# Audio tower on one core: small and large weight loads of the opening on two queues, and the first batch ahead of the weight preparation

## The reference

```
h = tokenizer(x)                        # frames * window -> DFT -> power -> mel
                                        #   -> log(mel + 1e-6) @ dct.T @ w_proj + b_proj
n = layernorm(h)
h = h + attention_block(n)              # rmsnorm * norm1_w; q, k, v = n @ wq, wk, wv (8 heads)
                                        # scores = q.k + (q.w_pos).basis + u.k + (v.w_pos).basis
                                        # softmax, @ v, @ wo + bo; rmsnorm; gelu(@ w1 + b1) @ w2 + b2
h = h + moe(layernorm(h))               # 16 experts, capacity 1000, plus a shared expert
```

## Time and profile before

| | us |
|---|---|
| median of 3 runs | 2097.63 |
| lowest and highest of the 3 | 2095.09, 2100.26 |
| the profiled execution | 2095.16 |
| its span, first to last instruction | 2093.5 |
| PE busy | 1937.0 (93% of the span) |
| DVE, ACT, POOL busy | 1351.9, 1070.5, 702.5 |

### The profile page before, as it was taken

One profiled execution on the slowest core, in us unless ns is written; L12 is line 12 of the kernel. 1 busy time (PEld: TensorE's weight loads), 2 busy tenths in 40 slices (PEclk: granted clock), 3 DMA queues, 4 the chain that ended last, 5 costly groups with the idle time before them and its releaser, 6 DMA issues. The chain is left out here.

```text
span 2093.5 us, 46401 instructions
## 1 busy us (share of the span) xinstructions
PE 1937.0 (93%) x13428; PEld 1660.4 (79%) x13428; DVE 1351.9 (65%) x3700; ACT 1070.5 (51%) x2588; POOL 702.5 (34%) x587
## 2 busy tenths in 40 slices
PE   2899999999999999999958899899999999999997
PEld 2788888888888788888747777788888888888886
DVE  2578878878878877877847777454555555555531
ACT  2687887887887887787732221222222222222221
POOL 0022222222222222222210002366566655566653
PEclk9899999999999999999979999999999999999999
DMA  5556656666666666666726333244445444444452
GB/s 153 161 160 173 192 168 172 191 169 173 189 170 173 187 172 173 186 174 173 194 74 162 98 102 97 56 82 88 85 88 98 90 84 78 78 78 81 81 94 20
DMA packets 318048, 272.95 MB, mean 130 GB/s; under 512 B 80732, under 2 KB 305326, under 8 KB 317998
## 3 DMA queue, kind: packets, MB, share of 16 engines
q1 hardware_dynamic: 238878, 235.53, 41.4%
q0 software_dynamic: 70656, 30.65, 9.9%
q10 hardware_dynamic: 8464, 6.15, 0.9%
HBM read 151.25 MB, written 120.54 MB: 130 GB/s over the span
## 5 line engine op out<-in xcount | busy, mean ns | idle before, releaser
L1208 POOL DMA_INDIRECT out<-ff_y,ff_idxs x128 | 261.8, 2045 | 244.7 <-DVE ff_y L1481 187.6
L1263 ACT ACTIVATE ff_sg<-ffp_g 128x500 f32<-128x500 f32 x192 | 112.9, 588 | 397.2 <-PE ffp_g L1593 397.2
L1195 POOL DMA_INDIRECT ff_xg<-xs_d,ff_idxg x128 | 204.3, 1596 | 284.5 <-issue 271.2
L524 ACT ACTIVATE sb_prob<-sb_ssb,sb_mx 125x250 f32<-125x250 f32 x512 | 253.1, 498 | 61.0 <-DVE sb_rinv L614 33.1
L1605 PE MATMUL ffp_d<-ff_wd,ff_wide 128*125 128x192 f32 x1536 | 261.2, 327 | 16.2 <-DVE ff_wide L1468 15.4
L1468 DVE TENSOR_TENSOR ff_wide<-ff_sg,ffp_u 128x500 f32<-128x500 f32 x192 | 129.4, 674 | 222.1 <-PE ffp_u L1593 222.1
L1605 PEld LDWEIGHTS ffp_d<-ff_wd,ff_wide 128*125 128x125 f32 x1536 | 247.8, 188 | 20.0 <-issue 18.4
L1593 PE MATMUL ffp_g<-ff_xsp,ff_wsp 128*128 128x500 f32 x960 | 251.2, 392 | 1.9 <-DVE ff_xsp L1345 1.6
L1593 PE MATMUL ffp_u<-ff_xsp,ff_wsp 128*128 128x500 f32 x960 | 248.9, 389 | 0.0
L822 PE MATMUL ps_qps<-sb_hsp,sb_wsp 128*128 128x250 f32 x1280 | 186.8, 293 | 31.5 <-DVE sb_hsp L728 22.8
L1593 PEld LDWEIGHTS ffp_g<-ff_xsp,ff_wsp 128*128 128x128 f32 x960 | 179.8, 189 | 39.8 <-issue 2.4
(11 more groups left out here) (189 smaller groups left out, 3562.6 us busy)
## 6 DMA issues: line engine op xcount, KB each, us to landing
bias_d<-sb_rsb SPq DMA_DIRECT2D x256, 219.6 KB
sb_bsk<-bias_d SPq DMA_DIRECT2D x256, 218.8 KB
hx_d<-sb_hx SPq DMA_DIRECT2D x32, 336.0 KB
sb_hxl<-hx_d SPq DMA_DIRECT2D x32, 336.0 KB
ff_wd<-WdT SPq DMA_DIRECT2D x16, 576.0 KB, 4.9
xs_d<-sb_xs SPq DMA_DIRECT2D x32, 238.0 KB
bias_d<-sb_rsb SPq DMA_DIRECT2D x256, 25.5 KB
sb_bsk<-bias_d SPq DMA_DIRECT2D x256, 25.4 KB
```

The lines of the kernel that those rows point to most:

```text
L524: a.activation(prob[:, s % 2, t], ssb[:, s % 2, t], ACT.Exp, bias=mx[:, s % 2, t:t + 1], scale=-1.0, accum_out=rs[:, t, s:s + 1]).then_inc ...
L1195: g.indirect_dma_start(xg[:, t], None, xs_d[:, :], bass.IndirectOffsetOnAxis(idxg[:, t:t + 1], 0), bounds_check=last).then_inc(gat, 16)
L1208: g.indirect_dma_start(out_d[:, :], bass.IndirectOffsetOnAxis(idxs[:, t:t + 1], 0), y[:, t], None, bounds_check=last, compute_op=ALU.add). ...
```

## The change

ACT issues 14 loads at its very start: eight small ones of the first stage (`dft`, `dct`, `w_proj`, `b_proj`, `melT` twice, `ident`, `n1w`) on a new semaphore `t_ld`, then `wqT`, `v` and the four of `w_pos`, still on `w_ld`. SP keeps the other 26, now with the large weights first and the biases `b2`, `bo` last; it waits for two memsets in place of three. POOL clears the tiles in another order, and waits for `w_ld` only after its first power. PE makes `wmel` first (`mel_mm`, `mel_in`), runs the first batch's DFT, mel and `wmel` products on `t_ld` alone, and then folds. ACT and DVE do their parts of the weight preparation inside the first batch, behind `hx` and behind the statistics. The folded products move from `tps` and `cps` to `cps` and `otps`, since `tps` now holds the first batch. The wait for `ini` (8 now) stands ahead of the first `qk`. In the other rounds nothing moves.

```
 def opening(bt):
     return isinstance(bt, int) and bt == 0
@@ sync: the order of SP's loads
-loads = [ident, dft, mel, mel, dct, wproj, b_proj, wqT, wo, w2, gate, n1w, n2w, b1, u, v]
...
+loads = []
+for name, (first, end) in COLS.items():
+    loads += [(wraw[:, 0, cols], w[name][0:128])]
+    loads += [(wraw[64 * i:64 * i + 64, 1, cols], w[name][128:D]) for i in range(2)]
...
-            sp.wait_ge(z_set, 3)
+            sp.wait_ge(z_set, 2)
             for dst, src in loads:
                 sp.dma_start(dst, src).then_inc(w_ld, 16)
+            sp.wait_ge(z_set, 7)
@@ scalar
+            for dst, src in ((dft[:], w["dft"]), (dct[:], w["dct"]), (wproj[:], w["w_proj"]), (wmel[MELS:MELS + 1], w["b_proj"]),
+                             (mel[0:BINS], w["melT"]), (mel[BINS:2 * BINS], w["melT"]), (ident[:], w["ident"]), (n1w[:], w["n1w"])):
+                act.dma_start(dst, src).then_inc(t_ld, 16)
+            act.wait_ge(z_set, 1)
+            act.dma_start(wqT[:], w["wqT"].rearrange("(p r) n -> r p n", r=128)).then_inc(w_ld, 16)
...
             a.preload_act_table_set(EXP_SET)
-            act.wait_ge(w_ld, W_LOADS)
+            act.wait_ge(t_ld, T_LOADS)
...
                         a.activation(hx[:, :, 0:D], bank2(tps, D, TP), ACT.Copy).then_inc(t_ev, 1)
+                        if opening(bt):
+                            weights_high()
@@ vector
                         v.tensor_scalar(t_v[:, NT:2 * NT], t_inv[:], EPS, None, ALU.add).then_inc(t_ch, 1)
+                        if opening(bt):
+                            weights_low()
@@ tensor
-            pe.wait_ge(w_ld, W_LOADS)
+            pe.wait_ge(t_ld, T_LOADS)
+            pe.wait_ge(z_set, 7)
+            m(qps[1][0:MELS, 0:D], dct[:], wproj[:], start=True, stop=True).then_inc(mel_mm, 1)
...
-            pe.wait_ge(ini, 9)
...
                 if p == 0:
+                    if opening(b):
+                        pe.wait_ge(ini, 8)
                     pe.wait_ge(t_ev, T_USES * (b + 1))
...
                         ins.then_inc(t_mm, 1)
+                        if opening(bt):
+                            fold()
```

More of the change, by code:

```diff
@@ L205, in tower @@
         zero_st = sem("zero_st")
+        t_ld = sem("t_ld")
+        mel_mm = sem("mel_mm")
+        mel_in = sem("mel_in")
         fold_mm = sem("fold_mm")
@@ L319, in load_shared @@
                     sp.dma_start(sh.xraw[half * 64:half * 64 + 64, 0, 1], xnT_d[128:D, 0:CHUNK]).then_inc(sh.x_ld[0], 16)
[L321 to L324, removed]
+            loads = []
+            for name, (first, end) in COLS.items():
+                cols = slice(first, end)
+                loads += [(wraw[:, 0, cols], w[name][0:128])]
+                loads += [(wraw[64 * i:64 * i + 64, 1, cols], w[name][128:D]) for i in range(2)]
+            for i in range(2):
+                for r in range(2):
+                    loads += [(braw[64 * r + 32 * i:64 * r + 32 * i + 32, i, 0:ND], w["basis"])]
+            loads += [
+                (ucol[:], w["u"]),
                 (wo[:], w["wo"].rearrange("(k p) n -> p k n", p=128)),
@@ L333, in _ @@
                           (bb[:, t, D:2 * D], w["bo"].partition_broadcast(TP))]
[L334 to L341, removed]
             def load_frames(b):
@@ L412, in _ @@
             g.memset(logmel[:], 1.0).then_inc(z_set, 1)
-            g.memset(vz[:], 0.0).then_inc(z_set, 1)
             g.memset(tiny[:], 1e-6).then_inc(z_set, 1)
             g.memset(power[:], -0.5).then_inc(z_set, 1)
-            pool.wait_ge(w_ld, W_LOADS)
+            g.memset(zeros[:], 0.0).then_inc(z_set, 1)
+            g.memset(vz[:], 0.0).then_inc(z_set, 1)
             pool.wait_ge(z_set, 7)
@@ L464, in _, with weights_high @@
             a = nc.scalar
+            for dst, src in ((dft[:], w["dft"]), (dct[:], w["dct"]), (wproj[:], w["w_proj"]), (wmel[MELS:MELS + 1], w["b_proj"]),
[3 more added lines that the diff above has]
+            act.dma_start(wqT[:], w["wqT"].rearrange("(p r) n -> r p n", r=128)).then_inc(w_ld, 16)
+            act.dma_start(vcol[:], w["v"]).then_inc(w_ld, 16)
+            for i in range(2):
+                for r in range(2):
+                    act.dma_start(wpz[64 * i:64 * i + 64, :, r, i], w["w_pos"].rearrange("(p i d) n -> i d p n", i=2, d=DK)[i]).then_inc(w_ld, 16)
             a.preload_act_table_set(EXP_SET)
-            act.wait_ge(w_ld, W_LOADS)
+            act.wait_ge(t_ld, T_LOADS)
             act.wait_ge(z_set, 7)
[L469 to L474, removed]
+            def weights_high():
+                act.wait_ge(w_ld, W_LOADS)
+                for k in range(2):
+                    a.activation(wsp[:, 2 * k, 0:ALL_COLS], wraw[:, k], ACT.Copy).then_inc(w_hi, 1)
+                act.wait_ge(fold_mm, 1)
+                for k in range(2):
+                    for i in range(2):
+                        a.activation(pos_cols(slice(0, 128), 2 * k, i), folded(i, k), ACT.Copy).then_inc(w_hi, 1)
             def shared_high():
@@ L566, in _, with weights_low @@
             v = nc.vector
-            dve.wait_ge(w_ld, W_LOADS)
+            dve.wait_ge(t_ld, T_LOADS)
             dve.wait_ge(z_set, 7)
[L569 to L579, removed]
+            dve.wait_ge(mel_mm, 1)
+            v.tensor_copy(wmel[0:MELS], qps[1][0:MELS, 0:D]).then_inc(mel_in, 1)
+            def weights_low():
+                dve.wait_ge(w_ld, W_LOADS)
+                v.tensor_copy(bz[:], braw[:]).then_inc(ini, 1)
+                for k, half in ((0, slice(0, 128)), (1, slice(64, 128))):
+                    dve.wait_ge(w_hi, k + 1)
+                    v.tensor_tensor(wsp[half, 1 + k, 0:ALL_COLS], wraw[half, k], wsp[half, 2 * k, 0:ALL_COLS].bitcast(F32), ALU.subtract).then_inc(ini, 1)
+                dve.wait_ge(fold_mm, 1)
+                v.tensor_copy(cq[:], qps[0][:, 0:PAIRS]).then_inc(ini, 1)
+                dve.wait_ge(w_hi, 6)
+                for k, half in ((0, slice(0, 128)), (1, slice(64, 128))):
+                    for i in range(2):
+                        v.tensor_tensor(pos_cols(half, 1 + k, i), folded(i, k)[half], pos_cols(half, 2 * k, i).bitcast(F32), ALU.subtract).then_inc(ini, 1)
             def pt_copy(b, h):
@@ L699, in body @@
                             v.bn_stats(t_stats[:, t], hx[:, t, 0:D]).then_inc(t_ch, 1)
-                        apart(dve, READY, (t_ch, b0 + 2))
+                        apart(dve, (t_ld, T_LOADS), (t_ch, b0 + 2))
                         for t in range(NT):
@@ L736, in _, with fold @@
             m = nc.tensor.matmul
-            pe.wait_ge(w_ld, W_LOADS)
[L738 to L746, removed]
-            pe.wait_ge(ini, 9)
-            pe.wait_ge(z_set, 7)
+            pe.wait_ge(t_ld, T_LOADS)
+            pe.wait_ge(z_set, 7)
+            m(qps[1][0:MELS, 0:D], dct[:], wproj[:], start=True, stop=True).then_inc(mel_mm, 1)
+            def fold():
+                pe.wait_ge(w_ld, W_LOADS)
+                for p in range(PAIRS):
+                    for k in range(2):
+                        for i in range(2):
+                            rows = slice(64 * i, 64 * i + 64)
+                            m(folded(i, k)[:, p], wqT[rows, p, k * 128:(k + 1) * 128], wpz[rows, p, 0, i], start=True, stop=True)
+                for p in range(PAIRS):
+                    ins = m(qps[0][:, p:p + 1], wpz[:, p].rearrange("d r i n -> d (r i n)"), vcol[:, p:p + 1], start=True, stop=True)
+                ins.then_inc(fold_mm, 1)
             def transposes(ps, src, s):
@@ L894, in body @@
                         pe.wait_ge(t_ev, T_USES * bt + 2)
+                        if opening(bt):
+                            pe.wait_ge(mel_in, 1)
                         ps = bank2(tps, D, TP)
```

12 lines of the change are left out of this document (7 added, 5 removed).

## The result

| | before | after |
|---|---|---|
| median, us | 2098.95 (4 runs, 2095.09 to 2100.44) | 2083.36 (4 runs, 2079.59 to 2088.32) |
| the profiled execution | 2095.16 | 2088.32 |
| its span | 2093.5 | 2086.7 |

The ratio is 0.9939, 95% interval 0.9922 to 0.9955: 12.8 us faster, with 9.4 to 16.4 as its interval. The two medians of the table lie 15.6 apart, which is inside it. The median of 2083.36 stands at the forecast of 2083. The profiled execution is the slowest of the four and shows only 6.8 us of gain in its span, so its opening is read first and its far end apart.

The account below looks back on a forecast made before the run. PE is busy 93% of the span; the opening's loads were taken as bound by issue on one queue. First `qk` 14.4 us earlier, less 0.7 for late frames, gives 13.7: from the median 2083.9, set at 2083, range 2076 to 2091.

Parts of the forecast that it names:

- The issue on SP: Opening, SP's queue: its 26 loads cost 14.2 us, the last issued at 16.0 in place of 23.08.
- `w_ld` full: Opening: all weight loads landed at 20.1, range 18.0 to 22.5, with `bb` last on few engines; chance 0.60 for 19 to 21.5.
- its two rows of 58 and 101: Profiled GB/s while `bb` loads were under way; four `bb` loads would take 6.5 us at 58 or 3.7 at 101.
- The small loads: Opening, ACT's queue: eight small loads, issued by 3.9, have landed at 6 to 8.
- the rival: Small loads queue beside large ones, `t_ld` fills at 16 or later, first stage sticks out: gain 5 to 9; chance 0.06.
- The preparation: Weight preparation after the loads: 8.16 us less 0.8 for the `wmel` product, so 7.4; `ini` full at 27.5.
- The end of the first stage: From weight preparation to the first `qk`: 4.42 us as before, so `qk` starts at 31.9, 14.4 earlier.
- The frames behind the zeros: Second batch's frames, queued behind 3.9 MB of zeros, land at 36 to 38.5 for use at 35.3: 0.7 lost.
- The sum: Whole kernel: 14.4 gained at the first `qk` less 0.7 for late frames, 13.7 us.
- shared issue: Rival: both queues share descriptor generation, `w_ld` full at about 24.6, gain 9.9, 2087.7 us; chance 0.11.
- Loads hidden at 18.0: Rival: loads land right behind their issue, `w_ld` full at 18.0 with `bb` hidden, gain 15.5, 2082 us; chance 0.13.
- The clock: Rival: PE's clock stays lower for longer from `qk` on, work takes 1.75 times as long, kernel slower; chance 0.04.

Follow-up runs that it names:

- Experiment 6: Changed kernel with nine loads used only by later stages (`wo`, `w2`, `gate`, `n2w`, `b1`, four `bb`) on their own semaphore, same order: 2082.69 us, 0.9948 of before.
- experiment 8: Changed kernel with late loads on their own semaphore and second frames ahead of the zeros: 2078.40 us (0.9924 of before); again 2077.92 beside the changed kernel's 2078.94.
- experiment 3: Changed kernel with all 40 loads on SP in the old order, so only the first batch moves ahead of weight preparation: 2087.65 us, 0.9959 of before.
- experiment 4: Changed kernel with the four 125-row loads of `b2` and `bo` first in SP's order instead of last: 2085.04 us, 0.9939 of before.
- Experiment 7: Changed kernel with only the second batch's frames loaded ahead of the zeros: 2082.79 us, 0.9953 of before.
- experiment 2: Changed kernel with weight preparation again ahead of the first batch, so only the loads are split over two queues: 2092.45 us, 0.9977 of before.

## Why the prediction was right, point by point

**The issue on SP**: right, 16.53 for 16.0. ACT's issues ended at 8.5 for 7.5: the eight small ones took until 4.4 for 3.9, and the four `w_pos` 3.0 for 2.6. Its table load hid under the wait for the small loads.

**`w_ld` full**: forecast 20.1, range 18.0 to 22.5; six profiles with this order of loads show 20.50 to 22.07. The mechanism was the one priced, `bb` last on few engines, and 20.1 was its mis-sized term, by 1.0. From the first `bb` issue at 14.42 it took 6.66; less the 1.5 that the prediction counts until the first bytes move, 375 KB in 5.16 us are 73 GB/s. That lies between its two rows of 58 and 101, nearer the slower. The faster row may hold other bytes, too: SP began to issue the first `w_pos` load at 10.82, so it isn't sure that at 11.5 `bb` was alone under way. Experiment 6 shows what the tail costs: loads needed early are in at 16.95 (15.18 and 17.30 in experiment 8), so 3 to 6 us of waiting are for biases that nobody reads yet. The share of 0.35 from 16 to 17 agrees with 5 of 16 engines, as the Trainium skill, "DMA: Bandwidth & Descriptors", § "Why a DMA increments its semaphore by 16 and not by 1", gives for 125 rows; the 18.6 that its figure for an engine led to is earlier than all six profiles, and the measurement decides. Whether the zeros, which are issued from 16.53 on, slowed its end was not separated.

**The small loads**: forecast 6 to 8, measured 9.12 to 9.67. The last was issued at 3.94, so it took over 5 us to land while the engines were filling up with the large weights. This looks like the mechanism of the rival, in small, but it isn't shown: in experiment 3 the same load, issued by SP at 6.69 with fewer large ones about, took 4.1 too. It cost nothing: the power was ready at 19.1, 2.0 before the weights. Even in experiment 4, where they came in at 14.41, the first stage did not stick out: `qk` is 2.65 later there, and `w_ld` 2.66.

**The preparation**: 7.35 for 7.4 (21.08 to 28.43). **The end of the first stage**: 4.52 for 4.42. `qk` at 32.95 for 31.9, and the difference of 1.0 is that of `w_ld`.

**The frames behind the zeros**: right in its mechanism. The prediction let the frames land at 36 to 38.5 for a use at 35.3, a wait of 0.7 to 3.2, and took 1.76 of idle time off it; that left a loss of 0 to 1.5, of which it took 0.7. The frames came at 36.7 to 38.1, as forecast, though their issue alone took 2.83 where it took 0.56 before. But `qk`, and with it their use, was 1.0 later. So the waits were 0.29, 0.86 and 1.69, each below 1.76, and the loss is 0: the second `qk` follows the first by 6.95 both in before (53.23 - 46.28) and after. Experiment 7 bears the rule out to a tenth of a microsecond.

**The sum**: 13.3 moved at `qk` against 13.7 forecast for the whole, 12.8 measured. Two errors of 1.0 and 0.7 nearly cancelled, and they hang together: the later `qk` is what made the wait for the frames free. That the median fell within 0.4 of 2083 is luck beyond that, since the runs themselves spread over 9 us.

**The rivals**: shared issue fell (experiments 2 and 3), though issues on both queues stretched by up to 16% while they overlapped, which no run explains. Loads hidden at 18.0 did not happen, though experiment 6 shows them so for the loads that matter. The clock did not make the kernel slower, and in the opening of the first two profiles the ten matmuls of `qk` take 2.5, 2.5, 1.4, 2.5 and 2.5 in turn, as in before. In the third the last of these takes 1.44, and its lead grows from 13.2 at the second `qk` to 15.9 at the last DFT; experiment 2's grows from 3.0 to 5.8 in the same way. So the clock moves an execution by some 3 us there, in either direction of a comparison. Near 1026 to 1110 the first profile lost another 6. With both, every run of the changed kernel still lies within 2076 to 2091.

## What to carry to other kernels

A wait on one semaphore for all weights makes the first step pay for the last. Ask of each load who reads it first, give early and late ones their own semaphore, and let the first batch run under the loads that it doesn't need: here the order of work brought 8.7 us and the second queue 3.9. Then look at what the earlier start meets next: here it was the second frames behind 3.9 MB of zeros, and a wait shortened in front of that queue brought nothing until the frames were moved ahead as well. A wait costs only what it exceeds of the idle time behind it; compare the distance to the next step before and after, not the wait itself, and look whether the engine ran at the same clock in both.

## What the runs showed of the hardware that was not expected

- Four loads of 125 rows at the head of one queue lengthened the issues of both SP (`wk` 3.43 for 1.73) and ACT (`v` 2.33 for 0.57) and delayed small loads of the other queue by 4.7 us. The same bytes cut to 112 and 13 rows did not.
- The granted clock reads 1.00 in the first stretches, as from 34 to 35 above, although ten matmuls of `qk` take 2.47 there and 1.43 later; the time of a known matmul is the better witness of the level.
- Behind the zeros SP's later issues stretched as well: the frames' took 2.83 in the changed kernel, 0.56 before and 0.54 in experiment 7, where it stands ahead of them.
- Profiles of one program differed by 17 us in how long PE stood at its lower level between 1026 and 1110, and by 6 to 7 us in what became of the lead there. For a change of 13 us in 2100 one profile's end says little; the landmarks right behind the change agree within 0.8 us.
